# Keys of five context tiles transposed in 32x32 blocks on VectorE and moved by on-chip DMA, instead of transposed on TensorE

## What is computed

```python
xn = layernorm(x, ln_x_g, ln_x_b)            # context, (2, 1024, 256)
ln = layernorm(latents, ln_l_g, ln_l_b)
kv = jnp.concatenate([xn @ Wkv, ln @ Wkv], axis=1)
k = kv[:, :, 0].transpose(0, 2, 1, 3)        # 16 heads of 64
qn = rmsnorm(q, qn_g) * scale
kn = rmsnorm(k, kn_g)
sim = jnp.einsum('bhid,bhjd->bhij', qn, kn)
attn = softmax(where(mask, sim, max_neg))
out = einsum('bhij,bhjd->bhid', attn, v) @ Wout + bout
```

## Time and profile before

| | us |
|---|---|
| median of 3 runs | 231.17 (231.15 to 231.9) |
| profiled execution, own time | 230.81 |
| its span from first to last instruction | 229.0 |
| TensorE busy in the span | 220.4 |
| DVE, ACT, POOL busy | 152.4, 154.6, 80.3 |

### The profile page before, as it was taken

One profiled execution on the slowest core, in us unless ns is written; L12 is line 12 of the kernel. 1 busy time (PEld: TensorE's weight loads), 2 busy tenths in 40 slices (PEclk: granted clock), 3 DMA queues, 4 the chain that ended last, 5 costly groups with the idle time before them and its releaser, 6 DMA issues.

```text
span 229.0 us, 4194 instructions
## 1 busy us (share of the span) xinstructions
PE 220.4 (96%) x1444; PEld 190.8 (83%) x1444; DVE 152.4 (67%) x352; ACT 154.6 (68%) x342; POOL 80.3 (35%) x132
## 2 busy tenths in 40 slices
PE   7899999999999999999999999999999999899984
PEld 6567678887788888988888989889999988799873
DVE  2899899998958777686766755566766752404431
ACT  4778778889895877777676567777777755314261
POOL 5288897860782746546060500000000010000300
PEclk9999999999999999999999999999999999999999
DMA  6591153200000000000000999600000000000000
GB/s 200 144 289 57 47 172 129 72 23 0 23 3 0 1 4 0 0 0 3 0 0 3 303 412 327 159 0 3 0 4 0 1 3 0 0 3 0 0 3 23
DMA packets 11252, 13.80 MB, mean 60 GB/s; under 512 B 1592, under 2 KB 9952, under 8 KB 10976
## 3 DMA queue, kind: packets, MB, share of 16 engines
q1 hardware_dynamic: 10680, 11.97, 16.3%
q10 hardware_dynamic: 552, 1.58, 2.0%
HBM read 13.15 MB, written 0.13 MB: 58 GB/s over the span
## 4 chain that ended last, share of the span: by engine, by line
PE 71%; DVE 16%; ACT 7%; issue 4%; POOL 1%; POOLq 0%; ACTq 0%; DVEq 0%
PE banks L1341 18%; PE banks L1191 14%; PE banks L1250 9%; PE banks L1282 8%; PE banks L1492 5%; DVE small L919 4%; DVE sk L931 4%; PE banks L1371 4%; PE banks L1364 3%; PE banks L1284 2%; PE banks L1413 2%; PE banks L1519 2%; DVE small L888 1%; DVE raw L882 1%; ACT knT L643 1%
## 5 line engine op out<-in xcount | busy, mean ns | idle before, releaser
L954 DVE TENSOR_TENSOR ptl<-banks,pth 128x512 fp32r<-128x512 f32 (+1 forms) x48 | 26.7, 557 | 24.1 <-ACT pth L679 23.2
L1341 PE MATMUL banks<-xnh,pth 128*128 128x256 f32 x128 | 37.6, 294 | 0.0
L1341 PE MATMUL banks<-xnh,ptl 128*128 128x256 f32 x128 | 36.3, 283 | 0.0
L1341 PE MATMUL banks<-xnl,pth 128*128 128x256 f32 x128 | 36.2, 283 | 0.0
L522 POOL TENSOR_TENSOR small<-small 128x16 f32<-128x16 f32 x7 | 20.4, 2913 | 31.7 <-DVE small L926 31.7
L679 ACT ACTIVATE pth<-banks 128x512 fp32r<-128x512 f32 (+1 forms) x48 | 23.7, 493 | 11.0 <-PE banks L1191 9.9
L626 ACT ACTIVATE sk<-banks 128x512 f32<-128x512 f32 x36 | 20.7, 601 | 11.8 <-PE banks L1250 11.3
L931 DVE TENSOR_TENSOR sk<-banks,small 128x512 f32<-128x512 f32 x36 | 23.0, 680 | 7.4 <-POOL small L522 7.3
L919 DVE TENSOR_REDUCE small<-sk 128x8 f32<-128x512 f32 x36 | 23.5, 677 | 5.0 <-ACT sk L626 5.0
L502 POOL COPY sp<-sp 128x64 f32<-128x64 f32 x16 | 3.8, 236 | 62.9 <-ACT sp L660 62.8
L1191 PE MATMUL banks<-ident,sp 128*128 128x128 f32 x144 | 24.2, 280 | 0.9 <-ACT sp L660 0.8
(11 more groups left out here) (198 smaller groups left out, 479.7 us busy)
## 6 DMA issues: line engine op xcount, KB each, us to landing
knT<-in_L_attn_qkv_kernel SPq DMA_DIRECT2D x1, 3072.0 KB, 12.0
raw<-in_ctx SPq DMA_DIRECT2D x16, 128.0 KB, 2.4
knT<-in_L_xattn_Wq SPq DMA_DIRECT2D x1, 1024.0 KB, 5.6
wv<-in_L_xattn_Wkv ACTq DMA_DIRECT2D x1, 1024.0 KB, 4.9
wout_sb<-in_L_xattn_Wout SPq DMA_DIRECT2D x1, 1024.0 KB, 5.3
knT<-in_L_attn_out_kernel SPq DMA_DIRECT2D x1, 1024.0 KB, 14.7
wraw<-in_L_xattn_Wkv ACTq DMA_DIRECT2D x1, 512.0 KB, 3.9
wraw<-in_L_xattn_Wkv SPq DMA_DIRECT2D x1, 512.0 KB, 5.3
```

The lines of the kernel that those rows point to most:

```text
L954: nc.vector.tensor_tensor(ptl[:, j0:j1, :], banks[:, t3_bank(u, c), 0:(j1 - j0) * P].rearrange("p (j r) -> p j r", j=j1 - j0), pth[:, j0:j ...
L1341: nc.tensor.matmul(banks[:, u_bank(u), 0:D], p_[:, j, :], x_, start=(j == 0 and i == 0), stop=False)
```

## The change

Five of the items (11 to 15, `BLOCKED`, tiles 1 to 5 of batch 1) are no longer transposed on TensorE. `key_blocks(i)` on DVE transposes `sk` (128x1024) in blocks of 32x32 and writes it into `knT`, not to the tile's own columns but to those of the next tile (of the last one: to those of tile 7). Since 32x32 blocks only turn within their 32 partitions, SP then moves 16 blocks of partitions and columns with 16 transfers of 32 partitions x 8 groups x 32 elements (128 bytes a piece) to the tile's own place. The transfers of an item start when `key_blocks` is done and when all of the item before have landed (`kq_landed`). ACT waits for all 80 of them ahead of the last item's `keys_out`, and so do `unit_high` and `logits` for batch 1. In the units concerned TensorE transposes the next tile ahead of `mix_transposed` and into the upper half of bank 5 instead of bank 1; the middle third of the probabilities goes to bank 2; and DVE does `xt_low` ahead of the first `probs_low`.

```diff
+    BLOCKED = range(ITEMS_A + 1, ITEMS - 2)
+    QD = P // 4
...
+            for i in BLOCKED:
+                sp.wait_ge(kb_ready, blocked(i + 1))
+                if blocked(i) > 0:
+
+                    sp.wait_ge(kq_landed, 256 * blocked(i))
+                t = (tile(i) - 1) % NT
+                for r in range(4):
+                    for c in range(4):
+                        sp.dma_start(knT[c * QD:(c + 1) * QD, 1, :, t * P + r * QD:t * P + (r + 1) * QD],
+                                     blocks_home(i)[r * QD:(r + 1) * QD, :, c * QD:(c + 1) * QD]).then_inc(kq_landed, 16)
             sp.wait_ge(k_ps, 2 * ITEMS)
...
             def keys_out(i, h):
-                act.wait_ge(kt_ps, 2 * i + h + 1)
+                act.wait_ge(kt_ps, 2 * by_matmul(i) + h + 1)
+                if i == ITEMS - 1 and h == 0:
+
+                    act.wait_ge(kq_landed, 256 * blocked(ITEMS))
...
-                if i < ITEMS:
+                if i < ITEMS and i not in BLOCKED:
                     keys_out(i, 0)
                     keys_out(i, 1)
...
+            def key_blocks(i):
+                dve.wait_ge(kn_ready, 2 * i + 2)
+                if i == BLOCKED[0]:
+
+                    dve.wait_ge(lns_ready, 1)
+                nc.vector.transpose(blocks_home(i), sk[:, i % 2, :].rearrange("p (g j) -> p g j", g=G)).then_inc(kb_ready, 1)
...
+                    if i in BLOCKED:
+                        xt_low(tile(i + 1))
                     probs_low(u, 0)
-                    if i + 1 < ITEMS:
+                    if i + 1 < ITEMS and i not in BLOCKED:
                         xt_low(tile(i + 1))
...
+                if i in BLOCKED:
+                    key_blocks(i)
                 if i + 2 < B * NT:
                     tile_center(i + 2)
...
+                    if i in BLOCKED:
+                        norm_transposed(tile(i + 1))
                     mix_transposed(u - 1)
-                    if i < ITEMS:
+                    if i < ITEMS and i not in BLOCKED:
                         keys_transposed(i, 0)
                         keys_transposed(i, 1)
-                    if i + 1 < ITEMS:
-                        norm_transposed(tile(i + 1))
+                        if i + 1 < ITEMS:
+                            norm_transposed(tile(i + 1))
                     probs_transposed(u, 1)
```

More of the change, by code:

```diff
@@ L134, in item, with by_matmul, blocked, blocks_home @@
             return n if n < QI else n + 1
+        def by_matmul(i):
+            return i - len([k for k in BLOCKED if k < i])
+        def blocked(i):
+            return i - by_matmul(i)
+        def blocks_home(i):
+            t = (tile(i) - 1) % NT
+            at = NT - 1 if i == BLOCKED[-1] else t + 1
+            return knT[:, 1, :, at * P:(at + 1) * P]
         def tile(i):
@@ L239, in perceiver_layer @@
         kt_ready = sem("kt_ready")
+        kb_ready = sem("kb_ready")
+        kq_landed = sem("kq_landed")
         qg_ready = sem("qg_ready")
@@ L346, in t1_bank, with t1_at @@
         def t1_bank(n):
-            return 1 if n > FA + 2 else 7 if n == FA + 2 or n % 2 else 5
+            return 5 if n > FA + 2 else 7 if n == FA + 2 or n % 2 else 5
+        def t1_at(n):
+            return D if n > FA + 2 else 0
         def t2_bank(i, h):
@@ L368, in t3_bank @@
         def t3_bank(u, c):
-            if u == 0 and c == 1:
+            if c == 1 and (u == 0 or ITEMS_A + u in BLOCKED):
                 return 2
@@ L439, in _ @@
             sp.dma_start(proj_sb, proj.rearrange("(c p) e -> p c e", p=P)).then_inc(w_tail["c"], 16)
[L440 removed]
+            sp.wait_ge(kt_ps, 2 * by_matmul(ITEMS))
+            sp.wait_ge(kb_ready, blocked(ITEMS))
             sp.dma_start(wout1_sb, Wout1.rearrange("(c p) r -> p c r", p=P)).then_inc(w_tail["ffn_a"], 16)
@@ L595, in xt_high @@
                     act.wait_ge(k_ps, 2 * item(n - 2) + 2)
-                nc.scalar.activation(xth[:, n % 2, :, :], banks[:, t1_bank(n), 0:D].rearrange("p (c r) -> p c r", c=DC),
+                nc.scalar.activation(xth[:, n % 2, :, :], banks[:, t1_bank(n), t1_at(n):t1_at(n) + D].rearrange("p (c r) -> p c r", c=DC),
                                      ACT.Copy).then_inc(xth_ready, 1)
@@ L623, in squares @@
                 act.wait_ge(k_ps, 2 * i + h + 1)
-                if i >= 2:
-                    act.wait_ge(kt_ps, 2 * (i - 1))
+                if i - 2 in BLOCKED:
+                    act.wait_ge(kb_ready, blocked(i - 1))
+                elif i >= 2:
+                    act.wait_ge(kt_ps, 2 * by_matmul(i - 1))
                 nc.scalar.activation(sk[:, i % 2, h * 512:(h + 1) * 512], banks[:, k_bank(i, h), :],
@@ L665, in unit_high @@
                 b, g = divmod(u, G)
-                act.wait_ge(kt_ready, 2 * (ITEMS_A if b == 0 else ITEMS))
+                act.wait_ge(kt_ready, 2 * (ITEMS_A if b == 0 else by_matmul(ITEMS)))
+                if b == 1:
+                    act.wait_ge(kq_landed, 256 * blocked(ITEMS))
                 act.wait_ge(qbd_ready, 4)
@@ L906, in xt_low @@
                 dve.wait_ge(xth_ready, n + 1)
-                full = banks[:, t1_bank(n), 0:D].rearrange("p (c r) -> p c r", c=DC)
+                full = banks[:, t1_bank(n), t1_at(n):t1_at(n) + D].rearrange("p (c r) -> p c r", c=DC)
                 if n == 0:
@@ L1205, in norm_transposed @@
                 if n > FA + 2:
-                    pe.wait_ge(kn_ready, 2 * item(n - 1) + 2)
+                    pe.wait_ge(max_ready, item(n) - ITEMS_A)
+                    pe.wait_ge(xtl_ready, n)
                 elif n == FA + 2:
@@ L1211, in norm_transposed @@
                     pe.wait_ge(xtl_ready, n - 1)
-                transposes(banks[:, t1_bank(n), :], lambda c: src[:, c * P:(c + 1) * P], DC).then_inc(xt_ps, 1)
+                transposes(banks[:, t1_bank(n), t1_at(n):], lambda c: src[:, c * P:(c + 1) * P], DC).then_inc(xt_ps, 1)
             def project(i, h, terms=(0, 1, 2)):
@@ L1221, in project @@
                 elif i > ITEMS_A + 1:
-                    pe.wait_ge(kt_ready, 2 * i)
+                    if i - 1 in BLOCKED:
+                        pe.wait_ge(kn_ready, 2 * i)
+                    else:
+                        pe.wait_ge(kt_ready, 2 * by_matmul(i))
                 elif i >= 2:
@@ L1256, in keys_transposed @@
                 pe.wait_ge(kn_ready, 2 * i + h + 1)
-                if i > 0 and (h == 0 or i < ITEMS_A):
+                if i > ITEMS_A:
+                    if h == 0 and i - 1 in BLOCKED:
+                        pe.wait_ge(ptl_ready, 3 * (i - ITEMS_A - 1) + 2)
+                    elif h == 0:
+                        pe.wait_ge(kt_ready, 2 * by_matmul(i) - 1)
+                elif i > 0 and (h == 0 or i < ITEMS_A):
                     pe.wait_ge(kt_ready, 2 * i - 1 + h)
@@ L1271, in logits @@
                 elif part == 0:
-                    pe.wait_ge(kt_ready, 2 * ITEMS_A if b == 0 else 2 * ITEMS)
+                    pe.wait_ge(kt_ready, 2 * ITEMS_A if b == 0 else 2 * by_matmul(ITEMS))
+                    if b == 1:
+                        pe.wait_ge(kq_landed, 256 * blocked(ITEMS))
                     pe.wait_ge(max_ready, u)
@@ L1311, in probs_transposed @@
                     pe.wait_ge(ptl_ready, 3 * u + c - (1 if c == 2 else 2 if c == 1 else 0))
+                elif ITEMS_A + u in BLOCKED:
+                    pe.wait_ge(ptl_ready, 3 * u + (0, -1, 1)[c])
                 elif 0 < u < G or u == G and c != 1:
```

## The result

The change makes the kernel slower: 238.65 us (median of four, 237.31 to 239.38) against 231.16 on the same chip (four, 230.79 to 231.9), a ratio of 1.031 [1.0274, 1.0348]. The forecast was 229.4, a gain of 1.8 us; it became a loss of 7.5.

The account below looks back on a forecast made before the run. TensorE, busy 96% of the span, was taken as the bound. Profiled 230.81 us, less 4.35 for five freed slots, plus 2.6 for late transfers, gave 229.1; the median's 0.36 made it 229.4, range 226.2 to 238.7.

Parts of the forecast that it names:

- the sum's T = 11.0: SP's time for one item's 16 transfers: 15 issue spacings plus the last landing, 11.0 us; up to 10.5 is hidden.
- issue spacing of 0.605 us: Time between SP's neighbouring transfer issues, taken from four on-chip 64-row transfers; upper end 0.73 us.
- one for one: At unit 7, each us the transfers end after ACT needs them costs one us of kernel time; 2.6 us forecast.
- landing of the last: Wait for an item's last transfer to land, taken as 1.9 us because the DMA engines idle in units 1 to 6.
- deadline: Instant in unit 7 when ACT, at the last item's `keys_out`, needs all 80 transfers landed: 127.02 us.
- The row that it took: Profile row of four on-chip 64-row transfers issued in 2.42 us, read as 0.605 us each.
- the late chain: Rival: T above 11.6 us, so lateness at unit 7 eats the gain; 238.7 us at 0.73 spacing; chance 0.26.
- all three main cases: Transfers hidden (226.8 us, chance 0.26), late by 0 to 5.8 us (around 229.4, 0.40), or later and slower (0.26).
- The slot: TensorE's eight key transposes, removed in five units: 0.87 us each by starts, 4.35 us in all.
- the 0.1 us of room: Before `values`, TensorE arrives 1.69 us into the unit and ACT's `uT` is done at 1.57: no new wait.
- the slow transpose: Rival: DVE's transpose takes 2.44 us instead of 1.2, delaying `key_scale` and `kl`; 230.6 us, chance 0.05.
- The small pieces: Rival: 128-byte pieces take twice 30 ns on the DMA engines, an item 17.3 us; 261 us, chance 0.03.

Follow-up runs that it names:

- rows128: Changed kernel with each of an item's 16 transfers taking 128 rows x 2 groups instead of 32 x 8, same bytes and pieces; 239.38 us, ratio 1.0347.
- from_hbm: Changed kernel with the 80 transfers reading rows of the context in HBM instead of the blocks on chip; 240.3 us, ratio 1.0393.
- pieces512: Changed kernel with each of the 16 transfers in pieces of 512 bytes instead of 128, same rows and bytes; 237.24 us, ratio 1.0254.
- eight: Changed kernel with eight transfers an item instead of 16, equal bytes, pieces of 256 bytes; 226.44 us, ratio 0.9787.
- four: Changed kernel with only items 11 to 14 by blocks, item 15 back on TensorE; 227.28 us, ratio 0.9825.
- diag: Changed kernel with each item's four diagonal blocks copied by POOL, SP issuing only the other 12 transfers; 226.34 us, ratio 0.9788.
- nowait: Changed kernel with blocks going by turns to tiles 7 and 6, so SP need not wait for an item to land; 233.33 us, ratio 1.0083.

## Why the prediction was wrong

**The step that failed is the sum's T = 11.0, and in it above all the issue spacing of 0.605 us.** The mechanism was the predicted one, to the place: one stall of ACT and TensorE at the start of unit 7, ended by a DMA, paid one for one. Its size was not: 10.3 us late instead of 2.6. The terms:

| | predicted | measured |
|---|---|---|
| chain start | 74.65 | 75.34 |
| issue spacing | 0.605 | 0.653 |
| landing of the last | 1.9 | 1.89 |
| T, five in all | 55.0 | 62.0 |
| end of the chain | 129.65 | 137.33 |
| deadline | 127.02 | 127.1 |

The spacing is that of the eight steps from 76.79 to 82.01. Of the 7 us in T it makes 75 x 0.048 = 3.6. Four long steps between issues make another 3.2: 1.87 us (82.01 to 83.88), 1.71, 1.12 and 1.05, less 0.65 each. The first three are the long issues beside the instruction packets; the sum had no term for them. The prediction itself said that 0.1 us in the spacing is 7.5 us in the end.

The row that it took had the answer and was misread. It divided the 2.42 us of four issues by four, but four issues hold four lengths and only three spacings, and the first of these issues was a short one. SP's timeline before, in narrow windows, shows the second with the third issue, and the third with the fourth:

```profile
33.51 1.24 SPq L430 DMA_DIRECT2D knT<-knT  x2
34.15 1.24 SPq L430 DMA_DIRECT2D knT<-knT  x2
```

The first spacing is 33.51 - 32.97 = 0.54, the second 34.15 - 33.51 = 0.64, and the third is 0.64 too (1.24 less a length of 0.60). With 0.64 the sum gives T = 15 x 0.64 + 1.9 = 11.5 and a chain that is 5.1 us late: 231.9, no gain. The prediction's reasons for where the spacing lies, the number of rows and both ends on chip, are refuted by `rows128` and `from_hbm`.

**The clock was not foreseen**: 1.6 us for the first scores after the stall, which the price "one for one" leaves out.

**The rival that came true** is the late chain, and its 238.7 is the measured time almost to the digit, but by other terms: it had 11.9 us of lateness from a spacing of 0.73, and got 10.15 of wait, 1.6 of clock, a start later by 0.6 and a gain larger by 0.5. That the figures meet is luck. Its condition, T above 11.6 from a spacing of 0.65, is what happened. Giving it 0.26 was too little: 0.57 and 0.65 decide between all three main cases, and the row read rightly lies beside 0.65. (The range's lower end has a slip as well: five times 1.04 less 0.87 is 0.85, not 0.6.)

**What was right.** The slot was taken as 0.87 us by starts, and 0.86 came in unit 1 and 1.00 in units 2 to 5: in unit 4 the next product, `project`, begins 97.23 - 95.14 = 2.09 us after the unit's start, and before it was 100.47 - 97.38 = 3.09. In front of `values` the 0.1 us of room was used up: TensorE's weight loads waited for `uT` once in each of the five units (waits, 65.5 to 125.6 us), though its matmuls stood still for no more than 0.1 us a unit.

```profile
PEld banks L1431 <- ACT uT L739: 1.6, 5, 0.3
```

`xth`, `kl` and `key_scale` fitted, `kl` with more room than was thought: the third matmul of the scores is the first that needs it, not the second (done at 99.98 in unit 4, used at 100.52). DVE's transpose took 1.24 us where 1.2 was taken:

```profile
83.88 1.24 DVE L982 STREAM_TRANSPOSE knT<-sk 128x1024 f32<-128x1024 f32 x1
```

The 2.5 us estimated from the Trainium skill (VectorE: DVE Perf Modes, The three transpose paths) did not come: the measurement decides, and the slow transpose falls.

**The small pieces** cost the kernel's time nothing. From 75 to 137 us the DMA queue's line (packets, MB, share of 16 engines) is

```profile
q1 hardware_dynamic: 21758, 2.63, 26.2%
```

that is 0.262 x 16 x 62 / 21758 = 12 ns a piece, under half of the 30 ns allowed, and engines idle for three quarters of the time. The Trainium skill (DMA: Bandwidth & Descriptors, Specifications) names 512 bytes as the least transfer for full rate, with a read-modify-write below it. A price of small pieces does show in engine time: `pieces512` moves the same bytes in 512-byte pieces, and its line from 75 to 134 us is

```profile
q1 hardware_dynamic: 6240, 2.56, 17.8%
```

0.178 x 59 = 10.5 us of each engine, against 0.262 x 62 = 16.2 with 128 bytes. Whether a read-modify-write makes this half more is not shown; it does not reach the kernel's time, as SP sets the pace.

Where SP's track is full of issues, the Trainium skill (Perfetto Trace Analysis, What "DMA-bound" means) says that large descriptors (here: pieces) are what matters. `pieces512` has them four times as large and its issue goes from 611 to 597 ns, so for this chain the number of transfers decides, as `eight` shows.

**What stays open:** what makes an issue cost 0.61 us here and 0.43 for the single loads of the earlier trace rows, since neither rows, pieces nor source do. Whether SP comes to an issue from a wait or straight from another issue has a part in it: the load of `wout_sb` took 0.60 us directly behind the train (`four`, `diag`), but before, where SP had been waiting, its timeline has

```profile
125.11 0.38 SPq L433 DMA_DIRECT2D wout_sb<-in_L_xattn_Wout  x1
```

That is not all of it, since the first issue of an item, after 1.9 us without one, still took 0.58 (88.45). Nor do three dimensions alone make an issue dear, as this load of 128x8x256 has them too. Open is also whether the instruction packets cause the long issues.

## What to carry to other kernels

Price a train of small transfers as issues times spacing, plus one landing for each wait in between, against the instant at which someone needs the last of them; count the issues, not the bytes. Take the spacing from the starts of neighbouring issues, not from the length of a group divided by its count. Where an item's train is longer than the beat in which items come, it falls behind by the difference each time, and the gain of the whole change hangs on the last one: drop an item, or a quarter of the issues, and it is hidden (`four`, `diag`). A stall of TensorE of 4.7, 6.2 or 10.15 us cost its length and 2.7, 2.8 or 1.6 us more here, as the granted clock was 1.00 again only some time after work had begun.

## What the hardware showed that was not expected

- An issue in such a train took SP 0.60 to 0.62 us (median) whether the transfer had 32 or 128 rows, pieces of 128 or 512 bytes, 32 or 64 KB, a source in HBM or on chip.
- Two to five issues in each train of 60 to 80 took 0.89 to 1.94 us, all 32 of them beside a DMA packet of the kind "instruction"; in `eight` these packets fell between the items, and no issue was over 0.73.
- The same load (`wout_sb`) took SP 0.38 us to issue after a wait and 0.60 directly behind the train.
- TensorE's granted clock was 0.50 after a wait of 10 us, and four matmuls that took 1.84 us before took 3.46; after a wait of 4.7 us (`nowait`) twelve others took 5.46 instead of 2.77.
- POOL copied a 32x256 block in 0.4 us (four in 1.77), beside its other work, at no cost to the time.
